# Attention with keys and values of two batches as seven block products, all queries at the layer's opening, and the value product two units later

## The reference

```
def _attn(xf, cond, Wq, Wk, Wv, Wo):
    xb = xf.reshape(BS, n // BS, d)
    q = (xb @ Wq).reshape(BS, -1, H, DH)
    k = (cond @ Wk).reshape(BS, -1, H, DH)
    v = (cond @ Wv).reshape(BS, -1, H, DH)
    att = jnp.einsum('bnhd,bmhd->bhnm', q, k) * DH ** (-0.5)
    w = jax.nn.softmax(att, axis=-1)
    o = jnp.einsum('bhnm,bmhd->bnhd', w, v).reshape(BS, -1, H * DH)
    return (o @ Wo).reshape(n, d)
...
for i in range(L):
    h = h + _attn(_ln(h, ln2_w[i], ln2_b[i]), cond, Wq[i], Wk[i], Wv[i], Wo[i])
    u = _ln(h, ln3_w[i], ln3_b[i]) @ geglu_w[i] + geglu_b[i]
    val, gate = jnp.split(u, 2, axis=-1)
    h = h + (val * gelu(gate)) @ ffo_w[i] + ffo_b[i]
```

## Time and profile before

| | us |
|---|---|
| median of three runs | 2401.38 (2400.44 to 2401.88) |
| profiled execution, its span | 2399.3 |
| PE busy, share | 2363.9, 99% |
| DVE busy, share | 1655.6, 69% |
| ACT busy, share | 1119.6, 47% |
| POOL busy, share | 667.3, 28% |
| head (sorting, first graph convolution) | 0 to 178 |
| openings of the layers | from 178.7, 722, 1260, 1800.5 |
| attention, then MLP of layer 1 | 739 to 1018, 1018 to 1265 |
| tail (second graph convolution) | from 2347 |

### The profile page before, as it was taken

The page is one execution under the profiler, slowest core; times in us unless marked ns, Lnnn a source line. Parts: engine busy times, 40 slices in busy tenths (PEclk is TensorE's granted clock), DMA queues, the critical chain, the costliest instruction groups (busy, mean ns, idle before and its releaser), DMA issues.

```text
span 2399.3 us, 32732 instructions
## 1 busy us (share of the span) xinstructions
PE 2363.9 (99%) x11966; PEld 1957.5 (82%) x11966; DVE 1655.6 (69%) x3168; ACT 1119.6 (47%) x2207; POOL 667.3 (28%) x441
## 2 busy tenths in 40 slices
PE   7899999999999999999999999999999999999999
PEld 5358888888888888888888888888888888888887
DVE  9986767785566767785566767785566766785554
ACT  9954434644334434644334444544334444554332
POOL 3111000066540000066540000066540000066540
PEclk9899999999999999999999999999999999999999
DMA  2031110122210110122211000122211100122222
GB/s 79 19 128 40 36 36 18 36 71 78 64 58 36 36 36 18 36 71 74 68 58 36 36 30 24 36 70 74 66 60 36 36 25 29 36 69 75 66 108 79
DMA packets 83306, 124.99 MB, mean 52 GB/s; under 512 B 5904, under 2 KB 63888, under 8 KB 78288
## 3 DMA queue, kind: packets, MB, share of 16 engines
q1 hardware_dynamic: 82864, 118.75, 14.9%
q10 hardware_dynamic: 288, 4.19, 0.4%
HBM read 116.36 MB, written 6.55 MB: 51 GB/s over the span
## 4 chain that ended last, share of the span: by engine, by line
PE 90%; DVE 5%; ACT 2%; POOL 1%; issue 1%; DMA 0%; SPq 0%; DVEq 0%; ACTq 0%
PE ps L2045 19%; PE ps L2047 19%; PE ps L2046 19%; PE ps L2391 7%; PE ps L2395 7%; PE ps L2393 7%; PE ps L2298 2%; PE ps L2315 2%; PE ps L2317 2%; DVE oh_d L1521 1%; DVE oh_d L1407 1%; PE ps L2312 1%; PE ps L2590 1%; ACT z L1045 0%; PE ps L2367 0%
## 5 line engine op out<-in xcount | busy, mean ns | idle before, releaser
L630 POOL TENSOR_TENSOR rstd<-veps,mhalf 128x1 f32<-128x1 f32 x48 | 26.0, 541 | 892.9 <-DVE veps L1314 892.9
L1976 DVE TENSOR_TENSOR h<-h,ps 128x512 f32<-128x512 f32 x256 | 168.8, 683 | 64.0 <-PE ps L2047 63.4
L734 POOL TENSOR_TENSOR f_lo<-ff,f_hi 128x512 fp32r<-128x512 f32 x128 | 169.0, 1332 | 156.2 <-ACT f_hi L1204 156.2
L996 ACT ACTIVATE v_hi<-ps 128x512 fp32r<-128x512 f32 x128 | 76.7, 599 | 285.1 <-PE ps L2047 285.1
L2045 PE MATMUL ps<-cond_hi,w_hi 128*128 128x512 f32 x512 | 202.1, 395 | 0.0
L2045 PE MATMUL ps<-w_hi,cond_hi 128*128 128x512 f32 x512 | 200.8, 392 | 0.0
L2045 PE MATMUL ps<-wf_hi,f_hi 128*128 128x512 f32 x512 | 199.6, 390 | 1.1 <-DVE ff L1960 1.0
L2047 PE MATMUL ps<-w_hi,cond_lo 128*128 128x512 f32 x512 | 200.3, 391 | 0.0
L2047 PE MATMUL ps<-cond_hi,w_lo 128*128 128x512 f32 x512 | 200.1, 391 | 0.0
L2046 PE MATMUL ps<-cond_lo,w_hi 128*128 128x512 f32 x512 | 200.1, 391 | 0.0
L2046 PE MATMUL ps<-w_lo,cond_hi 128*128 128x512 f32 x512 | 199.9, 390 | 0.0
(11 more groups left out here) (331 smaller groups left out, 6443.3 us busy)
## 6 DMA issues: line engine op xcount, KB each, us to landing
stage<-in_pieces SPq DMA_DIRECT2D x82, 512.0 KB, 3.3
stage<-in_condT SPq DMA_DIRECT2D x31, 1024.0 KB, 4.8
stage<-in_pieces SPq DMA_DIRECT2D x224, 128.0 KB, 2.6
at_s<-at_hi ACTq DMA_DIRECT2D x2, 2048.0 KB, 8.2
at_hi<-at_s SPq DMA_DIRECT2D x4, 1024.0 KB, 6.4
x<-in_x SPq DMA_DIRECT2D x2, 1024.0 KB, 7.0
out<-h SPq DMA_DIRECT2D x8, 256.0 KB, 2.0
bias_row<-in_rows SPq DMA_DIRECT2D x6, 256.0 KB, 3.6
```

Of the source, the lines that this page charges most:

```text
L734: pool.tensor_tensor(f_lo[q % 2][:, c, half * HALF:(half + 1) * HALF], ff[:, s % 2, :], bits(f_hi[q % 2][:, c, half * HALF:(half + 1) * HA ...
L1976: dve.tensor_tensor(h[:, t, :], h[:, t, :], ps[:, down_bank(q, t), :], ALU.add)\
```

## The change

- Keys and values of a group become seven block steps each (`kv_step`). A step is 12 matmuls of 256 columns: two halves of the output, two slices of the inputs, three matmuls. Steps 0 and 3 add up in bank A, 1 in B, 2 and 4 in C, then 5 and 6 in B again. The condition needs four differences of its blocks and seven split blocks (`cb`, one set, 7 x 512 numbers); the weights need four sums, as in the MLP.
- Out of PSUM come partial sums: `kv_first` (ScalarE), `kv_two`, `kv_five`, `kv_late` 0 to 2 and `kv_11_low` (VectorE), `kv_11_high`, `kv_high` 0 to 2 (ScalarE), `kv_low` 0 to 2 (GpSimd). Condition differences and low parts are on GpSimd, and no longer on VectorE.
- A group is now `value_units` and `key_units`: values of this group, then keys of the next. The value product of a unit comes two units after its scores (`pv_product(u - 2, ...)`), and there is one bank for it; the probabilities have two buffers.
- All queries are made at the opening: transposes and queries of the second four tiles follow those of the first. The queries of all tiles are kept in `z3`, and the query blocks are cut in two halves per group (`q_high`, `q_low`).
- Of the next layer's weights only the keys' are loaded during the MLP (and at its end the values'); those of queries and output are loaded whole (`load_whole`) at the end of the MLP and after the queries. Low parts of the values' weights are made at the opening.

Below, calls that stand on lines of their own are joined, and the extras of the last group are left out.

```diff
@@ TensorE @@
+def kv_step(t, kind, j):
+    n = kv_set(l, t, kind)
+    if kind == KEYS:
+        pe.wait_ge(c_lo, BLOCKS * (GROUPS * l + t) + j + 1)
+    if j == 0 and n:
+        pe.wait_ge(kv_11, n)
+    elif j == 1 and n:
+        pe.wait_ge(kv_sum, 5 * n)
+    elif j == 3:
+        pe.wait_ge(kv_p1, n + 1)
+    elif j == 4:
+        pe.wait_ge(kv_sum, 5 * n + 2)
+    elif j == 6:
+        pe.wait_ge(kv_sum, 5 * n + 4)
+    bank = (A_BANK, B_BANK, C_BANK, A_BANK, C_BANK, B_BANK, B_BANK)[j]
...
+            pe.matmul(to, l_hi, r_hi, start=(fresh and i == 0 and k == 0), stop=False, skip_group_check=True)
+            pe.matmul(to, l_hi, r_lo, start=False, stop=False, skip_group_check=True)
+            last = pe.matmul(to, l_lo, r_hi, start=False, stop=(k == 1), skip_group_check=True)
...
+def value_units(t):
+    kv_step(t, VALUES, 0); kv_step(t, VALUES, 1)
+    if t: pv_product(u - 2, t - 1, 2)
+    kv_step(t, VALUES, 2); kv_step(t, VALUES, 3)
+    p_transpose(u); s_product(u + 1, t, 1)
+    kv_step(t, VALUES, 4); kv_step(t, VALUES, 5)
+    if t: pv_product(u - 1, t - 1, 3)
+    kv_step(t, VALUES, 6)
+    p_transpose(u + 1); s_product(u + 2, t, 2)
+def key_units(t):
+    kv_step(t + 1, KEYS, 0); kv_step(t + 1, KEYS, 1)
+    pv_product(u - 2, t, 0)
+    if t: wo_product(GROUPS * l + t - 1)
+    kv_step(t + 1, KEYS, 2); kv_step(t + 1, KEYS, 3)
+    p_transpose(u); s_product(u + 1, t, 3)
+    kv_step(t + 1, KEYS, 4); kv_step(t + 1, KEYS, 5)
+    pv_product(u - 1, t, 1)
+    kv_step(t + 1, KEYS, 6)
+    p_transpose(u + 1); s_product(u + 2, t + 1, 0)
-v_product(None, 0, 0, V_BANK)
-if l: first_t2()
-v_product(None, 1, 0, V_BANK + 1)
-k_product(UNITS * l, 0, 0)
-v_product(None, 2, 0, V_BANK + 2)
-for p in range(PAIRS): q_product(0, p)
+for j in range(3): kv_step(0, KEYS, j)
+first_t2(0)
+for j in range(3, 5): kv_step(0, KEYS, j)
+for p in range(PAIRS): q_product(0, p)
+first_t2(1)
+for j in range(5, STEPS): kv_step(0, KEYS, j)
+for p in range(PAIRS): q_product(1, p)
+s_product(UNITS * l, 0, 0)
+pe.wait_ge(w_ok, attn_piece(VALUES, 1, l) + 1)
@@ SP @@
 wait_apart(sp, w_ok, FIRST_PIECES + PIECES * l)
 load_raw(1)
+sp.wait_ge(q_mm, 2 * FIRST * l + 2 * FIRST)
+load_whole(wo_raw, ...)
@@ GpSimd, end of a layer, then opening @@
+for n in range(3): cond_sum(g, n)
+cond_low(g, 0); cond_sum(g, 3)
+for j in range(1, BLOCKS): cond_low(g, j)
+first_rsqrt(2 * l + 2)
+for half in range(2): wq_low(l + 1, half)
+zero_q()
+for k in range(2): first_x2_low(0, k)
+kv_low(l, 0, KEYS, 0)
+first_rsqrt(2 * l + 1)
+attn_low(VALUES, 0, l); attn_low(VALUES, 1, l)
+for n in range(3): cond_sum(GROUPS * l + 1, n)
+for k in range(2): first_x2_low(1, k)
+for n in range(1, 3): kv_low(l, 0, KEYS, n)
@@ GpSimd, a group @@
+cond_low(g, 0); cond_sum(g, 3); cond_low(g, 1); kv_low(l, t, VALUES, 0); kv_low(l, t, VALUES, 1)
+cond_low(g, 2); cond_low(g, 3); kv_low(l, t, VALUES, 2); cond_low(g, 4); rsqrt(...)
+cond_low(g, 5); cond_low(g, 6); kv_low(l, t + 1, KEYS, 0); kv_low(l, t + 1, KEYS, 1)
+cond_sum(g + 1, 0); cond_sum(g + 1, 1); kv_low(l, t + 1, KEYS, 2); cond_sum(g + 1, 2)
@@ VectorE, opening @@
+kv_two(0, KEYS); kv_five(0, KEYS)
+for k in range(KC): first_x2_full(0, k)
+for k in range(2, KC): first_x2_low(0, k)
+kv_11_low(0, KEYS); kv_late(0, KEYS, 0)
+attn_sums(VALUES, 0, l)
+for t in range(FIRST): first_stats_of(2 * l + 1, t)
+first_aggregates(2 * l + 1); first_z2(2 * l + 1, range(FIRST))
+attn_sums(VALUES, 1, l)
+for i in range(2): q_low(0, i)
+for k in range(KC): first_x2_full(1, k)
+for k in range(2, KC): first_x2_low(1, k)
+kv_late(0, KEYS, 1); kv_late(0, KEYS, 2); maxima(UNITS * l)
@@ VectorE, a group: value_units, then key_units @@
+softmax(u); kv_two(t, VALUES); add_bias(t - 2); q_low(t, 1); o_part(u - 2, 2); kv_five(t, VALUES)
+kv_11_low(t, VALUES); pT_low(u); maxima(u + 1); softmax(u + 1); kv_late(t, VALUES, 0)
+kv_late(t, VALUES, 1); o_part(u - 1, 3); kv_late(t, VALUES, 2); pT_low(u + 1); maxima(u + 2)
+o_low(...); softmax(u); kv_two(t + 1, KEYS); o_part(u - 2, 0); q_low(t + 1, 0); kv_five(t + 1, KEYS)
+residual(t - 1, ...); kv_11_low(t + 1, KEYS); pT_low(u); z3_of(t - 1, ...); maxima(u + 1)
+kv_late(t + 1, KEYS, 0); kv_late(t + 1, KEYS, 1); softmax(u + 1); o_part(u - 1, 1)
+kv_late(t + 1, KEYS, 2); pT_low(u + 1); maxima(u + 2)
```

More of the change, by code:

```diff
@@ L412, in set_place, with loads @@
                 .rearrange("p (b n) -> p b n", n=256)
[L414 to L417 removed]
+        def loads(l, r):
+            before_it = (1, 1)[r % 2] + l * len([n for n in PLAIN_PIECES if n % 2 == r % 2])
+            here = PLAIN_PIECES + (KEY_PIECE if l == L - 1 else [])
+            return before_it + len([n for n in here if n <= r and n % 2 == r % 2])
         def short_set(l, q, c):
@@ L690, in _ @@
+            attn_low(KEYS, 0, 0)
+            attn_low(KEYS, 1, 0)
+            for n in range(3):
+                cond_sum(0, n)
+            cond_low(0, 0)
+            cond_sum(0, 3)
+            for j in range(1, 4):
+                cond_low(0, j)
             first_rsqrt(0)
             pool.wait_ge(agg_mm, NT)
+            for j in range(4, BLOCKS):
+                cond_low(0, j)
+            for half in range(2):
+                wq_low(0, half)
             pool.wait_ge(low_out, 32)
@@ L1133, in _ @@
-                for part in range(2):
-                    cond_high(1, 1, part, stage)
-                q_copy(0, 0)
-                act.wait_ge(qb_zero, 2 * l + 2)
-                q_high(0, slice(0, 1))
-                for p in range(1, PAIRS):
-                    q_copy(0, p)
-                q_high(0, slice(1, PAIRS))
-                unit(UNITS * l, GROUPS * l, 0, 0, 0, first=True)
-                for g in range(GROUPS - 2):
-                    body(g, g % 2)
-                body(GROUPS - 2, 0, ahead=False)
@@ L1146, in _ @@
-                body(GROUPS - 1, 1, last=True, ahead=False)
+                    first_x2_high(0, k)
+                kv_11_high(0, KEYS)
+                kv_high(0, KEYS, 0)
+                attn_high(VALUES, 0, l)
+                for p in range(2):
+                    q_copy(0, p)
+                attn_high(VALUES, 1, l)
+                for p in range(2, PAIRS):
+                    q_copy(0, p)
+                act.wait_ge(qb_zero, 3 * l + 3)
+                for i in range(2):
+                    q_high(0, i)
@@ L1869, in _ @@
-                if l:
-                    v_low(UNITS * l + 1, 1, 0, V_BANK + 1)
-                k_low(UNITS * l)
-                v_low(UNITS * l + 2, 2, 0, V_BANK + 2)
-                for part in range(2):
-                    cond_low(GROUPS * l + 1, 1, part, stage)
-                q_low(0, slice(0, 1))
-                q_low(0, slice(1, PAIRS))
-                maxima(UNITS * l)
-                unit(UNITS * l, GROUPS * l, 0, 0, first=True)
-                dve.wait_ge(row_in, 16 * l + 32)
```

1241 lines of the change are left out of this document (711 added, 530 removed).

## The result

| | before | after |
|---|---|---|
| median of 4 runs each, same chip | 2401.6 us (2400.4 to 2402.7) | 2676.4 us (2668.2 to 2685.3) |
| ratio, 95% interval | | 1.1145 (1.1119 to 1.117) |
| span of the profiled execution | 2399.3 us | 2675.6 us |

What follows compares the result with a forecast made beforehand. TensorE, busy 99% of the span, was taken as the bound: -62 us saved columns, +50 groups, +76 openings, +3 layer 0 make +67 on 2399.3, 2468 us as a median of runs. Range 2405 to 2545 us, 8 in 10.

Steps and rivals of the forecast that it cites:

- The saved columns: Key and value products on TensorE: 84 matmuls of 256 columns replace 48 of 512, 0.97 us less for each of 64, -62 us.
- Rival 3: Key and value steps on TensorE: each pays the change of weights, saving 26 instead of 62 us, 2504 us; 6 in 100.
- Steady groups: 28 middle groups of the attention stages: waits and contention add 1.8 us a group, +50 us (0 to +130).
- the late sum: Value half of a group: step 6 waits for a VectorE sum standing behind the softmax, 0.8 us.
- the condition blocks: Key half of a group: step 5 waits for low parts of condition blocks 5 and 6, behind GpSimd's root, 0.5 us.
- contention: Groups: VectorE operations lengthened where they meet GpSimd's, taken at 0.5 us a group, between 0 and 6.8.
- rival 2: Every group: GpSimd and VectorE lock each other, 4 us a group instead of 1.8, 2530 us; 17 in 100.
- The chain of the opening: Opening of each layer: second queries wait for low parts behind value weights and condition loads; TensorE stands 15 us, in two pieces.
- Q: Start of the first queries in a layer's opening; the second queries' input low parts were walked to Q+30.5 us.
- The clock: Openings: TensorE's clock goes down in gaps of 6 to 10 us, costing 2 us once a layer (0 to 3.4).
- The gap for the condition operations: Openings of layers 1 to 3: GpSimd's 11 condition operations, 14.3 us of work, fit in a 16 us gap.
- Layer 0: First opening: zeroing of query blocks and weight low parts stand ahead of the first low parts on GpSimd, +3 us.

Runs made afterwards that it cites:

- kernel with the cut groups: Changed kernel with GpSimd's condition sums, condition low parts and key/value low parts of the groups cut to 4 of 256 columns, openings untouched: 2561.6 us.
- the subtractions: Kernel before the change, with 17 GpSimd subtractions of 128x512 on a spare tile added in each of seven groups of a layer: 2464.0 us.
- memsets that leave the query low part at 626 ns: Kernel before the change, with 44 GpSimd memsets of a spare 128x512 tile added in each of seven groups of a layer: 2490.6 us.
- work was added against it: Changed kernel with 41 matmuls of 512 columns into a bank nobody reads added at each opening, where TensorE stood still: 2670.2 us.
- The expectation above: Changed kernel, value weights 1 and next conditions behind the second queries' input, late sum and key step 5 earlier, GpSimd idle for normalised tiles, layer 0 root earlier: 2649.9 us.

## Why the prediction was wrong

**The saved columns: right.** Steps run at 0.12 us start to start:

```profile
913.01 0.28 PE L2513 MATMUL ps<-cb,wk_hi 128*128 128x256 f32 x1
913.13 0.28 PE L2515 MATMUL ps<-cb,wk_hi 128*128 128x256 f32 x1
913.25 0.28 PE L2516 MATMUL ps<-cb,wk_lo 128*128 128x256 f32 x1
```

(kernel with the cut groups; the mean of all its steps is 0.1199). 84 x 0.1199 = 10.07 instead of 10.88 us, 64 times: -52 us, -62 predicted. Rival 3 is out.

**Steady groups, the step that failed.** I took 1.8 us a group: 0.8 for the late sum (0.83 measured), 0.5 for the condition blocks (0.50), and 0.5 for contention, "near the low end". Of the 4.8 us that a group now takes beyond TensorE's own 31.6 (32.4 in the kernel with the cut groups, less its one stop of 0.8), 36.4 - 32.4 = 4.0 go with GpSimd's operations: 0.5 us for the condition blocks and 3.5 in the place of my 0.5. In 28 groups that is 98 us instead of 14. The 3.5 hold the contention and, as at value step 4, GpSimd's results that come late, which my sum had only for the condition blocks; no run splits the two. That contention by itself can come near this size, two other numbers show: it keeps VectorE busy 7.3 us a group longer (31.1 against 23.8), and in the kernel before, where nobody waits for the subtractions, it costs 2.8 us a group. I had the upper end right in the text (6.8 us a group) and rival 2 right in kind (4 us a group, VectorE operations of double length; 17 in 100). What misled me was the row that I chose: the weight sums of the MLP stage, where GpSimd is busy too but VectorE's operations stand at places where GpSimd waits for them (103.6 us in all). The normalisation stands where GpSimd works., where 541 became 1825 ns, was the row nearest to the case. It also held more than I read in it: that operation, from 179.81 us on, met two memsets back to back (179.51 and 180.40, 0.95 us each) and waited for both.

The Trainium skill ("SBUF — State Buffer", Who interferes with whom) says that the second to start is blocked for the whole instruction of the first, and that VectorE operations with two inputs in SBUF contend only with GpSimd operations that read SBUF. Both agree here: pairs of 2.5 us against 0.61, and memsets that leave the query low part at 626 ns (627 before). The tile shown below goes beyond the first half of it: it waited not for one instruction but for four.

**The chain of the opening: right in its links.** Walked 30.5 us from Q, measured 31.6; TensorE's stops ahead of and behind Q are 4.07 + 5.57 + 4.77 + 1.24 = 15.7 us in layer 2, 17 a layer predicted. The clock fell as predicted (23.9 us at the low level in the openings of layers 2 and 3, 13.7 in that of layer 1); in layer 2, where work was added against it, it cost about 2 us, as I took. The gap for the condition operations I read 1 us too long: from the end of the last product to the root it is 15.0 us, not 16. The 14.3 us of work still fit in it. What I left out is that the lock works here too: GpSimd's share of the openings is 49 us in all, and the first groups of a layer have the stops of the steady ones. One piece of it, the normalised tiles ahead of the first transposes of layer 2 (VectorE, then GpSimd):

```profile
1402.48 2.33 DVE L1874 TENSOR_SCALAR o_full<-h,x_mv,x_veps 128x512 f32<-128x512 f32 x1
1404.73 5.29 DVE L1874 TENSOR_SCALAR full<-h,x_mv,x_veps 128x512 f32<-128x512 f32 x1
...
1410.99 0.54 DVE L1874 TENSOR_SCALAR p_exp<-h,x_mv,x_veps 128x512 f32<-128x512 f32 x1
...
1402.13 4.95 POOL L777 TENSOR_TENSOR wq_lo<-wq_raw,wq_hi 128x1024 fp32r<-128x1024 f32 x2
1407.01 0.95 POOL L736 MEMSET qbd_a<- 128x1024 f32 x1
1407.90 0.95 POOL L736 MEMSET qbd<- 128x1024 f32 x1
1408.79 0.95 POOL L736 MEMSET qbd_b<- 128x1024 f32 x1
```

The second tile, 0.54 us of work, waits not for one GpSimd operation but for four in a row. (The expectation above gives other durations for these tiles; the rows are right.)

**Layer 0: too small.** 15.2 us instead of 3. I had only the zeroing and weight low parts in it, not that the root stands behind the condition operations, nor that the load of the conditions waits for both halves of the key weights.

**The MLP stage: no term at all.** 7.6 + 7.6 + 7.9 = 23 us. I priced value weights in the opening and forgot that the same preparation, with its sums, stands at keys in the MLP stage, where it holds a stage buffer.

In sum, of the 208 us that were missing, 84 are the mis-sized contention term of the steady groups by itself (98 against 14), 23 the MLP stages, 12 layer 0, 10 the smaller saving. The remaining 80 are the openings, the first groups, the ends of layers and groups that fell to the low clock (38 to 39 us instead of 36.4; the first 20 intervals between output products, five a layer, average 37.3, which is 17 us more); they hold GpSimd's 49 us, but their parts weren't each measured.

## What to carry over

An engine that is idle is not free when its operations and the busy engine's keep each other waiting, as here (2.67 us for a pair that takes 0.61 alone). Before giving it work, list the busy engine's operations of the kinds that were stretched here (the normalisation, one tile in and out; the low parts, two tiles in from SBUF), and price each that can meet at the length of the helper's operation, not at its own. Of several rows on contention take the one whose place is like the new one's, and keep its size in the forecast until a row excludes it. Then go through every stage that prepares data for the changed one.

## What the hardware showed that I had not expected

GpSimd memsets at 73% of the time stretch the normalisation (352 to 559 ns), yet cost these groups nothing: the old order covers it. Subtractions of 1.1 us on average, at 54% of the time, cost 2.8 us a group. So the share of the time doesn't decide. Two things differ between the fillers: a memset is half as long, and it leaves VectorE's operations with two inputs at their length (626 against 997 ns for the query low part). Which of the two makes the difference in time was not tried. Nor is a wait limited to one operation: a tile of 0.54 us took 5.29 us behind four. And keeping the clock up with work for nobody gave back 6 us of the 26 that I had expected.
